# A decoder layer with a Mamba scan: the running sum of the states leaves one tile instead of two to TensorE, by a fourth adding transfer

## The reference, cut to what matters

```python
dA  = exp(delta * A)                 # per token, channel d (1024), state n (16)
dBu = delta * B * u
h   = dA_t * h + dBu_t               # scan over the 512 tokens
y_t = sum over n of h[d, n] * c_t[n] # the sum over the 16 states
y   = (y + u * D) * silu(res)
out = y @ W_out.T
```

## Time and profile before

| | |
|---|---|
| median of 3 runs | 2497.8 us (2497.44 to 2500.29) |
| the profiled execution, its own time | 2494.77 us |
| its span in the trace | 2493.0 us |
| PE, DVE, ACT, POOL busy, share of the span | 93%, 73%, 63%, 67% |
| mean granted clock of PE | 0.979 |

### The profile page before, as it was taken

The page is one execution under the profiler, slowest core; times in us unless marked ns, Lnnn a source line. Parts: engine busy times, 40 slices in busy tenths (PEclk is TensorE's granted clock), DMA queues, the critical chain, the costliest instruction groups (busy, mean ns, idle before and its releaser), DMA issues. The chain is left out here.

```text
span 2493.0 us, 38410 instructions
## 1 busy us (share of the span) xinstructions
PE 2328.9 (93%) x15232; PEld 1389.2 (56%) x15232; DVE 1830.0 (73%) x2160; ACT 1566.4 (63%) x2604; POOL 1675.3 (67%) x911
## 2 busy tenths in 40 slices
PE   8898999999999999899999989996799999999997
PEld 4565666566666665566656655563454554554543
DVE  4998898898898899889889878762465366356453
ACT  4786887878888878688788887742333433333332
POOL 1898889899899899789989988871333143143130
PEclk9999999999999999999999999997899999999999
DMA  6677978877878888787787787875000100000000
GB/s 205 142 151 167 223 153 178 216 170 172 219 160 186 207 165 174 163 214 159 168 224 170 167 216 151 209 179 187 1 32 4 34 34 1 34 34 1 17 17 17
DMA packets 104677, 331.67 MB, mean 133 GB/s; under 512 B 9699, under 2 KB 46947, under 8 KB 73779
## 3 DMA queue, kind: packets, MB, share of 16 engines
q0 software_dynamic: 27648, 201.34, 40.9%
q1 hardware_dynamic: 76851, 127.88, 15.1%
HBM read 108.30 MB, written 19.56 MB: 51 GB/s over the span
## 5 line engine op out<-in xcount | busy, mean ns | idle before, releaser
L1028 POOL TENSOR_TENSOR mamba_ring<-mamba_ring,mamba_c_row 128x1024 f32<-128x1024 f32 x512 | 1278.7, 2655 | 39.5 <-DVE mamba_ring L916 39.1
L916 DVE TENSOR_TENSOR_SCAN mamba_ring<-mamba_ring,ps 128x512 f32<-128x512 f32 x1024 | 1175.0, 1200 | 139.8 <-PE ps L456 134.1
L717 ACT ACTIVATE mamba_ring<-mamba_delta,mamba_a_neg 128x512 f32<-128x512 f32 x1024 | 659.4, 710 | 73.5 <-DMA mamba_ring<-mamba_ring 72.1
L456 PEld LDWEIGHTS ps<-shared,mamba_v_t 64*128 64x128 f32 x8192 | 499.5, 189 | 245.1 <-issue 148.1
L456 PE MATMUL ps<-shared,mamba_v_t 64*128 64x128 f32 x8192 | 581.1, 284 | 49.8 <-DVE mamba_ring L916 48.8
L1037 POOL DMA_DIRECT2D mamba_ring<-mamba_ring x192 | 180.3, 939 | 147.6 <-DMA mamba_ring<-mamba_ring 121.8
L1614 POOL TENSOR_TENSOR xf_pr<-xf_pr,xf_top 128x1232 f32<-128x1232 f32 x32 | 75.0, 2344 | 266.4 <-DVE xf_top L1536 266.4
L422 PE MATMUL ps<-mamba_xt,mamba_wres 128*128 128x512 f32 x512 | 239.7, 611 | 0.0
L365 PE MATMUL ps<-mamba_xt,mamba_wu 128*128 128x512 f32 x464 | 218.3, 614 | 5.6 <-DMA mamba_xt<-x_t 5.6
L890 DVE SCALAR_TENSOR_TENSOR mamba_u<-ps,mamba_wcv,mamba_u 128x511 f32<-128x511 f32 (+2 forms) x192 | 142.1, 740 | 74.3 <-ACT mamba_u L682 71.8
L508 PE MATMUL ps<-mamba_wout,mamba_u 128*128 128x512 f32 x352 | 168.0, 611 | 0.3 <-ACT mamba_gate L725 0.3
(11 more groups left out here) (129 smaller groups left out, 2781.7 us busy)
## 6 DMA issues: line engine op xcount, KB each, us to landing
mamba_ring<-mamba_ring POOLq DMA_DIRECT2D x192, 1024.0 KB, 7.7
mamba_c_row<-c_rows SPq DMA_DIRECT2D x32, 1024.0 KB, 11.6
mamba_wres<-w_res SPq DMA_DIRECT2D x64, 256.0 KB, 6.0
mamba_wu<-w_u SPq DMA_DIRECT2D x58, 256.0 KB, 4.0
mamba_xres<-x SPq DMA_DIRECT2D x32, 256.0 KB, 8.9
x<-mamba_xres SPq DMA_DIRECT2D x32, 256.0 KB, 4.4
mamba_xt<-x_t SPq DMA_DIRECT2D x7, 1024.0 KB, 14.2
xf_xn<-x SPq DMA_DIRECT2D x20, 256.0 KB, 4.0
```

Of the source, the lines that this page charges most:

```text
L456: m = nc.tensor.matmul(ps[:, 2 * s + i, tb * P:(tb + 1) * P], v_t[g % 2][i * H:(i + 1) * H, tb * P:(tb + 1) * P], diag_b[i * H:(i + 1) * H ...
L717: a = nc.scalar.activation(ring[:, q % NR, i, :], delta[:, d % EARLY, :], ACT.Exp, scale=a_neg[:, d, 2 * k + i:2 * k + i + 1])
L916: m = nc.vector.tensor_tensor_scan(ring[:, r, i, :], ring[:, r, i, :], both[:, bass.ds(i, T, 2)], 0.0, ALU.mult, ALU.add)
L1028: nc.gpsimd.tensor_tensor(ring[:, q % NR], ring[:, q % NR], c_row[:, 2 * k:2 * k + 2, :], ALU.mult).then_inc(c_done, 1)
```

## The change

A fourth transfer, `merge(g, 3)`, adds tile 6 into tile 7. It is half as large as the other three (one tile instead of two), waits for the landing of `merge(g, 2)`, and is issued by POOL behind `times_c` of step 4 of the next block, one step after `merge` 0 of that block. PE sums one tile (`SUMS = (7,)`) with 8 transposes instead of 16; this sum now waits for the landing of the fourth transfer, and stands at the end of step 7 instead of in step 6. The `y_transposes` stand at the end of step 0 of the block after, instead of at the end of step 7. The programs of ACT and DVE are as before, but for the semaphores: ring tile 6 is released by the fourth transfer, no longer by PE's sum.

```diff
-    MERGES = 3
-    SUMS = (6, 7)
+    MERGES = 4
+    SUMS = (7,)
...
-                if k == 6 and g >= 1:
-                    for e in SUMS:
-                        state_sum(g - 1, e)
...
                 if k == 7 and g >= 1:
-                    y_transposes(g - 1)
+                    for e in SUMS:
+                        state_sum(g - 1, e)
+                if k == 0 and g >= 2:
+                    y_transposes(g - 2)
...
+            y_transposes(NG - 2)
             pe.wait_ge(scanned, TOTAL)
...
             def merge(g, p):
 
-                src, dst = (g * NU + 2 * p) % NR, (g * NU + 2 * p + 2) % NR
-                pool.wait_ge(c_done, g * NU + 2 * p + 4)
+                n = 2 if p < 3 else 1
+                src, dst = (g * NU + 2 * p) % NR, (g * NU + 2 * p + n) % NR
+                pool.wait_ge(c_done, g * NU + 2 * p + 2 * n)
                 if p >= 1:
                     pool.wait_ge(merged[p - 1], 16 * (g + 1))
-                nc.gpsimd.dma_start(ring[:, dst:dst + 2], ring[:, src:src + 2], accum_op=ALU.add).then_inc(merged[p], 16)
+                nc.gpsimd.dma_start(ring[:, dst:dst + n], ring[:, src:src + n], accum_op=ALU.add).then_inc(merged[p], 16)
...
+                    if k == 4 and g >= 1:
+                        merge(g - 1, 3)
             merge(NG - 1, 2)
+            merge(NG - 1, 3)
```

## The result

The changed kernel takes 2751.64 us (median of 4 runs, 2748.16 to 2752.56), the one before 2499.05 us in the same session. The ratio is 1.1016, with a 95% interval of 1.0993 to 1.1039: 253 us slower. The profiled execution has a span of 2749.9 us; PE's mean granted clock is 0.932, before it was 0.979.

A forecast was written before the change was run, and what follows sets the result against it. PE and DVE together were taken to set the pace. Boundaries 150, ACT's tap 36, clock 20 and the end 3, less 7 for PE's gain, made 202 us: 2700 us on the median of 2497.8, range 2550 to 2810.

The forecast's parts named there:

- The place of the loss: PE's sum waits for the half transfer's landing, and DVE's gate behind it; 150 us over all block boundaries.
- In line behind merge 0: On POOL's queue the half transfer lands 2.65 us behind merge 0; 2700 us in all, chance 0.61.
- the two ends: Half transfer's landing: either 2.65 us behind merge 0, or, as if alone, 4.3 us behind its own issue.
- POOL catches up: POOL issues merge 0 as early as 2.75 us behind step 3's scan; otherwise boundaries cost 220 us, not 150.
- From landing to gate 3.2 us: From the half transfer's landing through PE's sum, ACT's copy and transposes back to DVE's gate: 3.2 us.
- The clock: PE's long wait halves its clock, costing some 3 us, once or perhaps twice a sequence: 20 us.
- the rival with falls nearly everywhere: In line, and PE drops to 1.2 GHz at most boundaries, 3 us more at some 45: 2830 us, chance 0.10.
- ACT's tap 36 us later: ACT's copy comes 1.3 us later against DVE, delaying the last tap in four blocks of 7 sequences: 36 us.
- Issue and traffic at nothing: The fourth transfer's issue on POOL, 39 us, hides in its wait for merge 0's landing; nothing in the sum.
- PE's gain: 8 fewer transposes in PE's queue: at most 4 us a sequence, some 30 in all; 7 us in the sum.
- The rival "as if alone": Half transfer lands without waiting for merge 0: 40 us at boundaries, perhaps 15 on ACT; 2550 us, chance 0.16.
- the list: Gate delays at one sequence's eight boundaries from d = 0: 0.8, 1.6, 3.8, 3.5, 0.6, 2.9, 0, 5.7 us.

## Why the prediction was right

Predicted were 2700 us with a range of 2550 to 2810; 2752 came. The chain of the loss was right, the size of its main term was not, and errors on the other side brought the number near. Point by point:

- **The place of the loss: right.** The wait in front of the sum went to 238 us in 60 waits, DVE stands in front of the gate. Taking PE's wait away takes 165 of 253 us with it.
- **In line behind merge 0: right, and the two ends were real.** At the boundary shown it lands 2.5 us behind merge 0, where 2.65 was worked out. With nothing ahead it takes 4.6 us (4.3 was worked out), and merge 0 behind it 9.0 at the least, where 6.9 was the least before. The Trainium skill ("DMA: Bandwidth & Descriptors", the section on two DMAs through the same engine) states that within one queue of one engine descriptors start in order but are pipelined. These runs agree: at none of the 62 boundaries does the half transfer land ahead of merge 0. Over the 62 boundaries the distance is 3.4 us on the mean, and 5 at d = 7, beside the c loads: the term of 2.65 was 0.8 us too small, some 50 us. At d = 7 the prediction also left out that POOL waits for merge 2 before it can issue the half transfer, 3.2 to 5.1 us in seven sequences.
- **POOL catches up: right.** It waits 298 us for scans, and merge 0 is issued 2.7 us behind the scan of step 3 at the median, 3.4 before (scan of step 4 starts at 826.46, issue at 828.64 in the block shown, where it was 721.78 and 724.32).
- **From landing to gate 3.2 us: too small.** The floor is 3.4, the mean 5.0. Two things were missed. The transposes back stand at the end of step 0, and at two boundaries of eight (into d = 3, and into d = 0) products with the output weights stand ahead of them. And the clock. At the 14 boundaries with the clock at full all the way it is 3.45 us on the mean. Together 1.8 us times 62 is 110 us.
- **The clock: the mechanism right, its frequency not.** I gave it one or two falls a sequence and 20 us, and the rival with falls nearly everywhere 0.10. In the changed kernel's Mamba part the clock fell 51 times (60 to 1900 us). 19 falls fewer in the run with fitted filler gave 23 us, 1.2 us a fall, against the 3 us that the rival had; the filler's own cost is in that figure, so a fall may cost more.
- **ACT's tap 36 us later: wrong.** DVE's wait for it is 62.8 us, 59.2 before. As I read it, the gate itself moved back by more than ACT did, so ACT is no later against DVE. The cost does exist, where PE doesn't wait (117 us in the run without PE's wait), with a cause that I hadn't named: the ring's tiles held by the late landing.
- **Issue and traffic at nothing: wrong by themselves.** The small unused transfer costs 9 us, the one of 512 KB 42, most of it in `make_diag`. In the changed kernel that instruction takes 17.9 us, 11 less than before: POOL has gaps there. Whether issue and traffic add to the 253 us or are covered by the wait, no run tells.
- **PE's gain:** 7 us were put in the sum, with "some 30 in all" as a bound. The run gave 7 us net, and with `make_diag` set aside the bound is about what it would give.
- **The rival "as if alone": its 40 us do not follow.** 3.4 us less at each of the eight boundaries leaves 0.4, 0.1 and 2.3 us a sequence of the list, some 22 us in all, and less at d = 7, where merge 0 alone takes 12.8 us. The rival didn't come, but by these figures its time was some 2535 us rather than 2550.

How the number came near is seen on DVE in the Mamba part (its wait at the gate before, then in the changed kernel, where the window is 60 to 1940 us):

```profile
DVE mamba_u L924 <- PE ps L487: 24.5, 15, 13.4
...
DVE mamba_u L925 <- PE ps L487: 312.6, 61, 13.6
DVE mamba_ring L917 <- PE ps L456: 104.8, 61, 13.2
```

Its wait at the gate went from 24.5 to 312.6 us, 288 more, where the boundaries and the clock together had 170 in the sum: this term was 118 us too small. Against it stand the tap, 36 us in the sum and 4 in the trace, the products of line 456, whose waits fell by 29 us, and `make_diag`, 11 us less. That the errors nearly cancel is luck.

The terms of the loss by the runs: 42 us for the transfer's presence, the places and the halved sum together, 45 us for the ring's tiles, 165 us for PE's wait with the clock in it, in the order in which they were taken away; together 252. `make_diag` is in them: 17 us more than before in the 42, and 27 us less in the changed kernel than in the run without PE's wait, so the 165 are what that wait costs net.

No version beats the kernel before. The one that gives the landing a step more is 81 us better than the change and still 6.9% slower than before, and the run with half the sum left out says that 7 us are all there is to win as long as `make_diag` stands where it does.

## What to carry to other kernels

Before moving work from a busy engine into a transfer, leave the work out once and see what its absence is worth: a share of 93% said nothing, 0.3% was the answer. Then compare the durations of the instructions, too, and not only the waits: an instruction that stretches hides in the busy time. Then count the distance, in steps, from the transfer's issue to the first instruction that waits for it, at the latency *behind what its queue already holds* (4.6 us alone, 7.8 here), and look at every semaphore that the landing releases, for the wait goes to the next of them when the first is taken away.

## What the hardware showed that I had not expected

A transfer half as large took as long to land as a whole one, 7.8 us both, because of its place in the queue. It took 4.6 us with nothing ahead of it. A granted clock that fell 51 times gave back little: filling PE's idle time with useless products took away 32 or 19 of the falls and was worth 14 or 23 us of 2750. And one DVE instruction on SBUF alone, 0.67 us long, took up to 9.3 us where POOL's products followed each other without a gap, and ended 0.56 us behind one of them every time.
